# Transposed rows read out by VectorE instead of ScalarE, and the second attentions' residual sums on GpSimd in two operations

## What is computed

```
x = x + 0.5 * ffn(layernorm(x))      # softmax attention with 16 heads of 16, two products, gelu
x = x + attn(layernorm(x))           # linear attention with 8 heads, no softmax
x = x + 0.5 * ffn(layernorm(x))      # the first step again, same weights

ffn(x): q, k, v = x@Wq, x@Wk, x@Wv   # split in 16 heads
        scores = einsum('bqd,bkd->bkq', q, k) / sqrt(256)
        out = einsum('bkq,bkv->bqv', softmax(scores, -1), v)
        z = l2_normalize(out @ Wo)
        z = l2_normalize(z @ Wff)
        return gelu(z)
```

## Time and profile before

| | before |
|---|---|
| median of 3 runs | 2878.8 us |
| the profiled execution | 2880.11 us |
| its span | 2878.3 us, 87462 instructions |
| granted TensorE clock, mean | 0.984 |
| VectorE busy | 2668.2 us |
| ScalarE busy | 2713.5 us |
| TensorE busy | 2668.9 us |
| GpSimd busy | 865.7 us |

### The profile page before, as it was taken

The page is one execution under the profiler, slowest core; times in us unless marked ns, Lnnn a source line. Parts: engine busy times, 40 slices in busy tenths (PEclk is TensorE's granted clock), DMA queues, the critical chain, the costliest instruction groups (busy, mean ns, idle before and its releaser), DMA issues.

```text
span 2878.3 us, 87462 instructions
## 1 busy us (share of the span) xinstructions
PE 2668.9 (93%) x35680; PEld 1073.0 (37%) x35680; DVE 2668.2 (93%) x5390; ACT 2713.5 (94%) x5031; POOL 865.7 (30%) x1389
## 2 busy tenths in 40 slices
PE   5899999999999999999999999999989899998987
PEld 2233443434434344344443443333323333333422
DVE  4999898998989989899899999999999999999997
ACT  3999999999999999999999999999999999999997
POOL 2324204333143331432424313132331313233111
PEclk8999999999999999999999999999999999999999
DMA  5231242323422334123341243422324342232440
GB/s 125 51 81 29 52 104 50 72 44 60 105 38 53 75 60 102 31 53 84 60 96 32 52 92 60 93 59 56 81 44 101 60 98 54 56 80 45 86 89 16
DMA packets 151363, 192.90 MB, mean 67 GB/s; under 512 B 34001, under 2 KB 85713, under 8 KB 150962
## 3 DMA queue, kind: packets, MB, share of 16 engines
q1 hardware_dynamic: 150386, 186.13, 31.6%
q0 software_dynamic: 576, 1.18, 0.3%
HBM read 36.18 MB, written 16.78 MB: 18 GB/s over the span
## 4 chain that ended last, share of the span: by engine, by line
PE 35%; ACT 31%; DVE 26%; issue 6%; POOL 1%; SPq 1%; DMA 0%; DVEq 0%; ACTq 0%; POOLq 0%
ACT exp_ring L593 25%; DVE exp_ring L678 21%; PE ring L784 12%; PE ring L838 10%; PE o_acc L849 10%; PE ring L889 2%; ACT w_xn L604 2%; ACT xn_T L612 1%; DVE bn_stats L718 1%; ACT kq_stage L627 1%; DVE w_xn L695 1%; ACT ring L599 1%; DVE v_now L751 1%; ACT L604 1%; SPq L430 1%
## 5 line engine op out<-in xcount | busy, mean ns | idle before, releaser
L678 DVE TENSOR_SCALAR_CACHE_REDUCE exp_ring<-ring 128x1024 f32<-128x1024 f32 x2048 | 2410.0, 1214 | 117.9 <-PE ring L838 109.5
L593 ACT ACTIVATE exp_ring<-exp_ring,neg_max 128x1024 f32<-128x1024 f32 x2048 | 2333.0, 1143 | 89.8 <-DVE exp_ring L678 87.2
L838 PE MATMUL ring<-kq_stack 128*32 128x512 bf16 x16384 | 1175.2, 383 | 124.3 <-DVE exp_ring L678 81.7
L849 PE MATMUL o_acc<-exp_ring,v_scaled 128*32 128x512 f32 x8192 | 1080.1, 600 | 34.7 <-POOL v_scaled L546 25.1
L838 PEld LDWEIGHTS ring<-kq_stack 128*32 128x32 bf16 x16384 | 406.7, 96 | 1038.4 <-DVE exp_ring L678 417.9
L546 POOL TENSOR_TENSOR v_scaled<-v_now,exp_rsums 128x64 f32<-128x64 f32 x512 | 150.1, 293 | 1764.3 <-DVE exp_rsums L688 1746.5
L593 ACT ACTIVATION_READ_ACCUMULATOR exp_ring<-exp_ring,neg_max 128x1 f32 x2048 | 387.9, 189 | 0.0
L849 PEld LDWEIGHTS o_acc<-exp_ring,v_scaled 128*32 128x32 f32 x8192 | 252.7, 111 | 253.9 <-POOL v_scaled L546 43.8
L784 PE MATMUL ring<-ffn_wo_wowff,o_T 128*32 128x256 f32 x4096 | 244.1, 380 | 15.4 <-DVE o_T L685 14.1
L784 PE MATMUL ring<-xn_T,ffn_wqkv 128*32 128x512 f32 x2048 | 249.0, 607 | 8.0 <-DVE exp_ring L678 6.7
L784 PEld LDWEIGHTS ring<-ffn_wo_wowff,o_T 128*32 128x32 f32 x4096 | 133.1, 110 | 125.1 <-DVE exp_ring L678 26.1
(11 more groups left out here) (99 smaller groups left out, 1249.2 us busy)
## 6 DMA issues: line engine op xcount, KB each, us to landing
kq_stack<-kq_parts SPq DMA_DIRECT2D x2030, 64.0 KB, 2.4
x_post<-in_L_attn_x SPq DMA_DIRECT2D x8, 1024.0 KB, 8.6
x_slots<-x_post SPq DMA_DIRECT2D x8, 1024.0 KB, 5.4
x_prep<-x_slots SPq DMA_DIRECT2D x8, 1024.0 KB, 8.7
x_post<-x_slots SPq DMA_DIRECT2D x8, 1024.0 KB, 5.8
x_prep<-in_L_attn_x SPq DMA_DIRECT2D x7, 1024.0 KB, 9.1
out<-x_post SPq DMA_DIRECT2D x7, 1024.0 KB, 5.7
kq_stack<-kq_parts POOLq DMA_DIRECT2D x18, 64.0 KB, 4.6
```

What stands on the lines that cost most here:

```text
L593: nc.scalar.activation(e, e, ACT.Exp, bias=negmax[:, i % NM:i % NM + 1], scale=-1.0, accum_out=sums[:, g % EG, c:c + 1]).then_inc(exp_done, 1)
L678: nc.vector.tensor_scalar(E[:, (g % EG) * HQ + c, :].rearrange("p (b n) -> p b n", b=NB), ps, -1.0, None, ALU.mult, ALU.min, accum_out=neg ...
L838: last = mm(ps[k:k + COLS, n, :], kq[:, 0, c, j * P + k:j * P + k + COLS], kq[:, 1, c, n * BANK:(n + 1) * BANK], start=True, stop=True)
L849: last = mm(O[32 * c:32 * c + 32, n, :], vsc[a][:, g % EG, c, :], E[:, (g % EG) * HQ + c, n * BANK:(n + 1) * BANK], start=(a == 0 and j == ...
```

## The change

- `xt` is read out by VectorE (`tensor_copy`) in place of ScalarE's copy, in all sixteen phases. It signals `xt_dve`; TensorE's waits for it go along.
- `x1` of the phases 8 to 14 runs on GpSimd: it halves `w_xn` in place (`tensor_scalar`), waits for that with the new semaphore `half_done`, and adds it to `x_post` (`tensor_tensor`). The phases 0 to 7 and the last one keep VectorE's one operation.
- Places, leads and gaps get other numbers.

```diff
         "START": {
-            "xn": (34.1, 34.4, 36.4, 40.8, 43.1, 46, 50.4, 53.7),
-            "xt": (41.6, 57.3),
-            "qk": (63, 69, 71.8, 74),
-            "v": (88.6, 92.2, 97.1),
-            "setup": (61.4,),
+            "xn": (36.1, 36.4, 37.6, 43.2, 43.9, 45.4, 52, 54.8),
+            "xt": (55.6, 60.1),
+            "qk": (60.2, 68, 68.2, 72.9),
+            "v": (77.5, 84.2, 86.5),
+            "setup": (64.9,),
...
         "PLAIN": {
-            "u": (8.7, 10.9, 12.4, 21.6, 29.9, 42.2, 55.8, 58.2),
-            "u_norm": (63.4,),
-            "w_norm": (66,),
-            "gelu": (67,),
-            "x1": (69.8, 70.4, 72, 72.3),
+            "u": (8.8, 10.8, 12.3, 21.3, 29.5, 42.6, 55.6, 58.3),
+            "u_norm": (59.1,),
+            "w_norm": (66.5,),
+            "gelu": (67.6,),
+            "x1": (68.6, 68.9, 72.7, 80.1),
...
-            "xn": (35.1, 35.9, 42.1, 45.5, 46.3, 46.8, 47, 47),
-            "xt": (62.2, 66.6),
-            "qk": (76.9, 84.2, 90.1, 101.7, 17.9, 25.6, 33.3, 37.3),
+            "xn": (44.7, 44.7, 46, 48.2, 49, 49.1, 50.6, 51.3),
+            "xt": (60.6, 68.2),
+            "qk": (77.5, 82.5, 88.8, 100.3, 17.6, 25.8, 33.5, 36.5),
...
-            "load_xp": (3.6,),
-            "stack1": (5.9,),
-            "load_xr": (7.8,),
-            "stack2": (40,),
-            "stack3": (81.5,),
-            "stack0": (107.7,),
-            "store": (113.4,),
+            "load_xp": (7.6,),
+            "stack1": (16.6,),
+            "load_xr": (8.9,),
+            "stack2": (44.8,),
+            "stack3": (78,),
+            "stack0": (120.2,),
+            "store": (113.1,),
...
         "LINEAR": {
-            "x1": (35.6, 36.3, 36.7, 37.3),
+            "x1": (35.2, 36, 36.5, 36.9),
...
-            "xt": (45.4, 47.1),
+            "xt": (43, 43.2),
...
-    GAP = {'gram': 0.5, 'y': 0.5, 'VK': 0.5, 'G': 0.5}
+    GAP = {'gram': 0.5, 'y': 0.5, 'VK': 0.5}
     LEAD = {"sp": {},
-            "pe": {"xt": -0.5},
-            "act": {"qk": 1.0, "u": 1.0, "xt2": 1.5, "gram": 1.0, "weights": 5.5, "G": 1.0, "xt": 0.5},
-            "dve": {"ln_stats": -1.0, "z": -2.0, "w_norm": 0.5, "ln2_stats": 0.5, "H": -0.5, "VK": -0.5, "T": 0.5},
-            "pool": {"recip": 0.5, "xbias": 4.5, "qk": -0.5, "xn2": -1.5, "u_norm": -0.5, "w_norm": 0.5, "x1": 1.5}}
+            "pe": {},
+            "act": {"qk": 1.0, "u": 1.0, "xt2": 1.5, "gram": 1.0, "weights": 8.0, "G": 1.5, "H": 0.5, "xt": 3.5},
+            "dve": {"ln_stats": -1.0, "z": -2.0, "w_norm": 0.5, "ln2_stats": 0.5, "VK": -0.5, "T": 0.5, "u_norm": -0.5},
+            "pool": {"recip": 0.5, "xbias": 3.5, "qk": -0.5, "u_norm": -1.5, "w_norm": 1.0, "x1": 0.5}}
...
+                elif kind == "x1" and not is_linear(p) and p < PHASES - 1:
+                    pool.wait_ge(xr_loaded, (p + 1) * 16)
+                    pool.wait_ge(gelu_done, chunk(p, i))
+                    w, x = wb[:, i * CT:(i + 1) * CT, 0:D], xr[:, i * CT:(i + 1) * CT, :]
+                    nc.gpsimd.tensor_scalar(w, w, 0.5, 0.0, ALU.mult, ALU.add).then_inc(half_done, 1)
+                    pool.wait_ge(half_done, chunk(p - B, i))
+                    nc.gpsimd.tensor_tensor(x, x, w, ALU.add).then_inc(x1_done, 1)
...
-                elif kind == "xt":
-                    if p >= 1:
-                        act.wait_ge(filled["qk"], nth("pe", "qk", p - 1, 7))
-                        act.wait_ge(filled["v"], nth("pe", "v", p - 1, 3))
-                    nc.scalar.copy(XT[:, i, :].rearrange("p (b n) -> p b n", b=NB), ps).then_inc(xt_act, 1)
...
-                elif kind == "x1":
+                elif kind == "x1" and (is_linear(p) or p == PHASES - 1):
...
+                elif kind == "xt":
+                    if p >= 1:
+                        dve.wait_ge(filled["qk"], nth("pe", "qk", p - 1, 7))
+                        dve.wait_ge(filled["v"], nth("pe", "v", p - 1, 3))
+                    nc.vector.tensor_copy(XT[:, i, :].rearrange("p (b n) -> p b n", b=NB), ps).then_inc(xt_dve, 1)
```

More of the change, by code:

```diff
@@ L51, in build_macaron @@
         "START": {
-            "ln_stats": (4.8, 16.7, 17.2, 20.8, 22.5, 23.3, 24.3, 25),
-            "ln_aggr": (29.2,),
-            "ln_rstd": (33.8,),
-            "xn": (34.1, 34.4, 36.4, 40.8, 43.1, 46, 50.4, 53.7),
-            "xt": (41.6, 57.3),
-            "qk": (63, 69, 71.8, 74),
-            "v": (88.6, 92.2, 97.1),
-            "setup": (61.4,),
-            "weights": (109.7, 116.5, 117.8, 122.1),
-            "stack0": (69.4,),
-            "load_xp": (47.7,),
+            "ln_stats": (4.8, 16.9, 17.2, 20.3, 23.5, 23.8, 26, 26.1),
@@ L63, in build_macaron @@
+            "ln_aggr": (29.4,),
+            "ln_rstd": (31.6,),
+            "xn": (36.1, 36.4, 37.6, 43.2, 43.9, 45.4, 52, 54.8),
[3 more added lines that the diff above has]
+            "setup": (64.9,),
+            "weights": (103.3, 106.3, 107.5, 114.2),
+            "stack0": (77.5,),
+            "load_xp": (50.4,),
         },
         "PLAIN": {
-            "recip": 5.1,
+            "recip": 5.2,
             "av": 9.1,
@@ L117, in build_macaron @@
[L117 to L124, removed]
+            "z": 4.3,
+            "u": (10.4, 11.6, 15.3, 16.2, 17.5, 21.3, 25.4, 27.2),
+            "u_norm": (27.3,),
+            "w_norm": (31.3,),
+            "gelu": (32.7,),
+            "x1": (35.2, 36, 36.5, 36.9),
+            "ln2_stats": (36.6, 38, 38.4, 38.9, 39, 39, 39.1, 39.2),
@@ new lines, in build_macaron @@
+            "ln2_aggr": (41.2,),
+            "ln2_rstd": (42.6,),
+            "xn2": (42.8, 42.9, 43.7, 45.4, 45.7, 46, 49.2, 50.5),
+            "gram": (52.3, 58.3),
+            "xt2": (67, 101.1),
+            "T": (63.8,),
+            "VK": (70.9,),
+            "G": (76.5,),
+            "H": (87.6,),
+            "xbias": (89, 89.2, 107.5, 111.1),
+            "y": (104.6, 109.3, 116.3, 120.3),
+            "ln_stats": (3.9, 12.5, 13.1, 15.6, 16.1, 17.8, 22.2, 23.3),
+            "ln_aggr": (27,),
@@ L125, in build_macaron @@
+            "ln_rstd": (29.7,),
+            "xn": (30.7, 32.1, 32.8, 33, 33.7, 33.8, 33.9, 34.6),
+            "xt": (43, 43.2),
+            "qk": (79.1, 81.1, 94.7, 97.9, 32.1, 35.9, 38.4, 41.8),
+            "v": (112.8, 124.7, 127.2, 4.2),
+            "load_xp": (12.1,),
+            "stack1": (63.3,),
+            "load_xr": (69.9,),
+            "stack2": (70.2,),
+            "stack3": (75.1,),
+            "stack0": (81.5,),
+            "store": (129.1,),
         },
         "TAIL": {
-            "u": (7.9, 8.9, 14.5, 30.4, 31.7, 51.3, 53.3, 67.3),
@@ L128, in build_macaron @@
[L128 to L133, removed]
+            "u": (8.5, 11.2, 15.7, 33.6, 38, 52.7, 60.9, 71.6),
+            "u_norm": (16.6, 74.7),
+            "w_norm": (35.5, 83.2),
+            "gelu": (72.3, 109.5),
+            "x1": (91, 104.5, 109.1, 116.9),
+            "load_xr": (13.1,),
+            "store": (123.5, 139),
@@ L652, in _ @@
             for (kind, p, i), _ in ORDER["dve"]:
-                if kind in ("tile", "u", "T", "VK", "H", "y") or (kind, p, i) in FIRST_SPLITS or (
+                if kind in ("tile", "u", "T", "VK", "H", "y", "xt") or (kind, p, i) in FIRST_SPLITS or (
                         kind == "v" and (kind, p, i) not in ON_ACT):
```

42 lines of the change are left out of this document (11 added, 31 removed).

## The result

Over 20 runs of each kernel the one after takes 2883.91 us (median), the one before 2879.22. The ratio is 1.0015, with a 95% interval of 1.0008 to 1.0021: 0.15% slower, within the 0.2% that the prediction counts as no change, where it forecast 0.44% faster. The interval lies wholly above 1, so the change goes the other way than forecast, if by little. The profiled span is 2884.0 us against 2878.3.

The account below looks back on a forecast made before the run. No single bound: TensorE in linear phases, ScalarE before the gelu in plain ones. Terms -10.8, -4.0, +2.0, -0.5, +0.5 gave -12.8 us: 2880.11 to 2867.3, 2866 on the median's scale; own range 2858 to 2874, overall 2848 to 2884.

Parts of the forecast that it names:

- Phases 1 to 8: -0.5 each: Linear phases: TensorE loses 0.7 us of waits for ScalarE's xt, VectorE gives back a little; -4.0 us in all.
- VectorE becomes the bound of the linear phases: Rival: 2.28 us of copies in one piece at tile 43, uncovered by TensorE's ring slots; +9.4 us, 2888; chance 0.10.
- VectorE, behind TensorE there, gives back a little: Linear phases: VectorE's added copies reduce TensorE's 0.7 us gain only slightly, leaving -0.5 us a phase.
- Phases 9 to 14: ScalarE's stretch shortens by 1.80; VectorE doesn't step in: Plain phases, 82 us stretch: VectorE's work becomes 78.0, below ScalarE's 80.1; 6 x -1.8 = -10.8 us.
- the -2.11 of x1's wait: Plain phases: VectorE's 2.11 us wait for the gelu before x1 goes; used only in the bound of -2.4 each.
- o_T and v_scaled come together, no cost booked: Plain phases behind the gelu: v_scaled after two GpSimd chunks near 2110.7, o_T near 2110.9, so TensorE loses nothing.
- the 1.5 named as the sign against it: Plain phases near the gelu: TensorE should show no wait for v_scaled over 1.5 us.
- phase 0: First phase: VectorE gains xt, keeps x1 and has 2.40 us idle in all; +2.0 us (0 to 2.3).
- START and phase 15: Beginning: xt on the way to the first qk, +0.5 us. Last phase: x1 away, -0.5 us (0 to -4.5).
- the price of x1 on GpSimd: Half 0.65, sum 1.2, semaphore about 0.1: 1.95 us a chunk, 28 chunks, 55 us on GpSimd.
- no slowing of VectorE by it: GpSimd's new work was expected not to slow VectorE's tile operations; nothing booked.
- The busy sums: Whole kernel: ScalarE busy about 29 us less, VectorE about 19 more, GpSimd about 55 more.

Follow-up runs that it names:

- e1: Changed kernel's engines for xt and x1, with the places, leads and gaps of the kernel before (START as changed); 2904.62 us, ratio 1.0086 to the kernel before.
- e3: Kernel before's places (START as changed), xt on VectorE in all phases, x1 left on VectorE; 2890.2 us, ratio 1.0037 to the kernel before.
- e2: Changed kernel's places and leads without the moves: xt on ScalarE at its old places, x1 on VectorE, START as before; 2892.21 us, ratio 1.0045.
- e4: Kernel before with only x1 of phases 8 to 14 moved to GpSimd, xt on ScalarE, old places; 2887.69 us, ratio 1.0027.
- f1: Changed kernel with xt on VectorE only in phases 10 to 15; START and everything linear in the order of before; 2877.44 us, ratio 0.9993.
- f4: Like f1, but only the second half of xt on VectorE, the first on ScalarE; 2876.97 us, ratio 0.999.
- f3: Changed kernel with GpSimd's x1 put behind v_scaled in its queue; 2888.23 us, ratio 1.003.
- g2: f1 with TensorE making the scores of tiles 70 to 75 twice in phases 9 to 15, same values; 2874.32 us, ratio 0.9982.
- g1: f1 with x1 back on VectorE, all four chunks behind tile 73; 2882.34 us, ratio 1.0009.
- g4: f4 with x1 back on VectorE, all four chunks behind tile 73; 2886.7 us, ratio 1.0024.

## Why the prediction was wrong, by its own steps

**"Phases 1 to 8: -0.5 each", measured +0.7 each.** The rival "VectorE becomes the bound of the linear phases" is what happened, around xt (e1, e3 against e2, e4, f1). "VectorE, behind TensorE there, gives back a little" was the step that failed. The 2.28 us of copies were booked at 0.2 (0.5 of TensorE's 0.7 was kept) and the rival was given 0.10, because VectorE is idle 15 us in such a phase. But of the 20 us around xt it has only 2.76 idle before, and the copies leave 0.76. The rival's reason, one piece that three ring slots can't cover, isn't the one: with two tiles between the copies most of the loss is there too (e1). ScalarE's relief bought nothing, since ScalarE waited for VectorE's tiles. The size came out below the rival's in part because the clock's fall near the gelu was 3.4 us long in five of after's phases (183.9) and 6.8 in phases 4 and 7 (185.5 and 185.3), and 6.8 in four of before's (183.9 to 184.3): part of what VectorE cost came back there. At like length, phase 4 of both, it is 185.5 against 184.2, the 1.3 from which the rival was said to decide.

**"Phases 9 to 14: ScalarE's stretch shortens by 1.80; VectorE doesn't step in", measured 0.9 without falls.** ScalarE did set the stretch, but the check was made over 82 us at once, with x1's 2.44 taken off on one side of the gelu and xt's 2.28 put on the other. Cut at 2098, the rows had the answer: VectorE 62.21 of 63.00, 0.79 us idle. The first copy, 1.14 us, doesn't fit where ScalarE frees 0.90; with both copies moved at the old places the gelu even starts 0.4 later (e3). The second copy alone gives the 0.9 (f4 against e2), the first 0.3 at most. Behind the gelu the -2.11 of x1's wait was rightly left out of the sum; ScalarE sets that stretch (f3).

**TensorE's clock was not in the sum at all.** Phases 9 and 14 lost 1.7 us each to it, which took 3.4 of the 5.4 us that six phases had gained. g2 gives it back. With it the parts add up: the start of the gelu, 75.1 us behind it, 1.7 for x1 on VectorE at the new places, and the late falls.

**"o_T and v_scaled come together, no cost booked".** As it turned out TensorE waits 2.41 us for v_scaled, more than the 1.5 named as the sign against it. GpSimd's side was right: v_scaled ends 5.1 us behind the gelu's start, 5.0 booked. VectorE's was not: o_T was taken to come 1.05 us sooner, with both copies (2.28) set against x1's wait, but only the second stands there (which gives 2.19), and o_T was done 2.27 us sooner in the phase (at 2117.31 in after, 2111.98 before). The cost is nothing all the same (f3: same 166.9 without that wait).

**Right:** phase 0 (+1.9 for +2.0), START and phase 15 within 0.5, the price of x1 on GpSimd, no slowing of VectorE by it. The busy sums came out smaller than forecast, ScalarE -19.0 for -29, VectorE +11.8 for +19, GpSimd +49 for +55. They had been counted at the price of an operation in its engine's sequence, while the page unites overlapping records; no run separates the two. That 2883.91 lies just inside the stated range of 2848 to 2884 is luck: its upper end was set by rivals that didn't happen, and a loss in the linear phases met a fifth of the gain forecast for the plain ones.

## What to carry to other kernels

When work moves from one full engine to another, compare the receiver's idle time with the moved piece in the very stretch where it lands, tens of microseconds at most, and don't set savings from the far side of a wait against it. Setting two tiles between the pieces saved little here (1.0 us of loss in place of 1.3), because the stretch around them was full. When the parts of a change don't seem to add up, cut the phases at a point that all kernels share, as the gelu's start was here, before calling it interplay. And look where TensorE's granted clock falls: the same fall is free or costly by what TensorE is asked for next, so a change that costs nothing by every engine's sum can move it into a product that others wait for.

## What the runs showed of the hardware

In most phases with a gelu the granted clock goes to 0.50 for 3.4 or 6.8 us behind TensorE's idle time around it, though TensorE is busy 92% of the span. In phase 14 of after TensorE had 7.07 busy us in the 12.50 before the fall, and the qk product, of which the start fell into it, took 2.30 us. Plain phases whose fall begins by 98.6 us (the latest early one, e3's phase 9) or that have none stay within 0.2 us of the kernel's shortest length. Those where it begins at 101.4 or later take 1.4 to 2.9 us more (after, e4, f1, f3, g1). In e1 and g4 all six begin at 100.9 or later, and there is no short phase to compare with. The Trainium skill (TensorE: Matmul & The Clock Gate, HAM oscillation) warns that idle gaps bring the clock down and that the matmuls behind them start slow. g2, whose gap is partly filled and whose plain phases have no fall, agrees; but phases 12 and 13 of after have no fall with the gap as it was. What a fall costs here is decided by the work behind the gap. What decides within one kernel whether a phase's fall comes at 95, at 102 or not at all, with the same code in each, stays open.
